# A graph and attention layer on one core: a new opening in which rows are normalised by pairs, TensorE turns most row tiles, and weights load late

## The reference

```
deg = max(count of edges per dst, 1)
xn  = layernorm(x)
x1  = x + (xn @ W1.T + b1 + (segment_sum(xn[src], dst) / deg) @ W2.T + b2)          # graph part
        + (relu(q) . (v_pad^T relu(k)) / normaliser) @ proj.T + proj_bias            # linear attention, 16 heads
          with q, k, v = xn @ qkv_weight.T
x2n = layernorm(x1)
pooled = softmax-weighted mean of x2n over all rows ; the gate picks 2 of 8 experts from it
out = x1 + sum over the 2 experts of g * gelu(gelu(x2n @ w1 + b1) @ w2 + b2)
```

## Time and profile before

| what | value |
|---|---|
| median of three runs | 1469.49 us |
| profiled execution | 1467.96 us, span 1465.9 us |
| busy, of the span | TensorE 93%, VectorE 63%, GpSimd 56%, ScalarE 42% |
| granted TensorE clock, mean | 0.967 |
| first tile's k on TensorE | 21.62 us |
| first gather, last gather issued | 167.7 us, 1156.9 us |

### The profile page before, as it was taken

One profiled execution on the slowest core, in us unless ns is written; L12 is line 12 of the kernel. 1 busy time (PEld: TensorE's weight loads), 2 busy tenths in 40 slices (PEclk: granted clock), 3 DMA queues, 4 the chain that ended last, 5 costly groups with the idle time before them and its releaser, 6 DMA issues.

```text
span 1465.9 us, 22487 instructions
## 1 busy us (share of the span) xinstructions
PE 1364.1 (93%) x7532; PEld 613.0 (42%) x7532; DVE 928.9 (63%) x2122; ACT 622.1 (42%) x1025; POOL 818.7 (56%) x880
## 2 busy tenths in 40 slices
PE   6899999998999999799699699889999889999997
PEld 3454433444444444344244244333434344444443
DVE  7797412115777777577477567746667466776677
ACT  6687412121444444243334234332434336555554
POOL 4542477777677777777777777777777400000000
PEclk9999999999999999899899899989999989999999
DMA  9999799997778787778787777878778541223322
GB/s 271 306 216 222 189 248 250 246 254 231 213 239 254 239 251 239 237 238 254 223 251 240 241 231 238 253 224 251 237 239 250 174 144 39 97 94 114 114 86 100
DMA packets 167029, 309.19 MB, mean 211 GB/s; under 512 B 72019, under 2 KB 74605, under 8 KB 166677
## 3 DMA queue, kind: packets, MB, share of 16 engines
q0 software_dynamic: 62560, 205.05, 47.2%
q1 hardware_dynamic: 36112, 58.90, 12.7%
q10 hardware_dynamic: 68260, 44.01, 11.6%
HBM read 255.02 MB, written 40.02 MB: 201 GB/s over the span
## 4 chain that ended last, share of the span: by engine, by line
PE 37%; POOL 34%; issue 12%; DVE 4%; DMA 1%; ACT 1%; SPq 0%; DVEq 0%; ACTq 0%; POOLq 0%
POOL ring L709 34%; PE bank L755 10%; PE bank L760 10%; PE bank L756 10%; PE bank L826 2%; PE bank L844 1%; PE bank L845 1%; DVE ring L2079 1%; PE bank L956 1%; DMA ring<-table,src_col 1%; PE bank L767 1%; PE bank L967 1%; PE bank L1005 0%; DVE work L2089 0%; DMA b1t<-in_L_ffn_b 0%
## 5 line engine op out<-in xcount | busy, mean ns | idle before, releaser
L709 POOL DMA_INDIRECT ring<-table,src_col x782 | 748.6, 957 | 255.7 <-issue 249.9
L755 PE MATMUL bank<-wts,xT 128*128 128x512 f16 x588 | 225.9, 384 | 13.4 <-DMA xT<-xT 5.7
L756 PE MATMUL bank<-wts,xT 128*128 128x512 f16 x588 | 226.1, 385 | 0.0
L826 PE MATMUL bank<-ring,hot 128*32 128x512 f16 x1560 | 123.8, 398 | 57.1 <-DMA ring<-table,src_col 51.8
L755 PE MATMUL bank<-wts,work 128*128 128x512 f16 x392 | 154.5, 394 | 2.0 <-ACT work L1297 1.4
L756 PE MATMUL bank<-wts,work 128*128 128x512 f16 x392 | 153.8, 392 | 0.0
L760 PE MATMUL bank<-wts,xT 128*128 128x512 f16 x588 | 152.9, 383 | 0.0
L1186 ACT ACTIVATE units<-bank 128x512 f16<-128x512 f32 x65 | 38.8, 598 | 212.0 <-PE bank L826 147.7
L1589 DVE SCALAR_TENSOR_TENSOR units<-bank,units 128x512 f16<-128x512 f32 x65 | 44.8, 689 | 124.0 <-ACT units L1186 123.2
L760 PE MATMUL bank<-wts,work 128*128 128x512 f16 x392 | 102.5, 385 | 0.0
L1718 DVE TENSOR_TENSOR work<-work 128x512 f16<-128x512 f32 x28 | 19.4, 692 | 125.8 <-ACT work L1251 125.8
(11 more groups left out here) (290 smaller groups left out, 2554.6 us busy)
## 6 DMA issues: line engine op xcount, KB each, us to landing
x_rows<-work ACTq DMA_DIRECT2D x51, 256.0 KB
ring<-table,src_col POOLq DMA_INDIRECT x782
work<-in_x ACTq DMA_DIRECT2D x48, 256.0 KB
ring<-x_rows SPq DMA_DIRECT2D x12, 1024.0 KB, 5.1
out_x<-ring SPq DMA_DIRECT2D x12, 1024.0 KB
table<-xT SPq DMA_DIRECT2D x45, 256.0 KB, 4.6
ring<-in_x SPq DMA_DIRECT2D x42, 256.0 KB, 4.1
xT<-in_L_mix_qkv_weight SPq DMA_DIRECT2D x2, 1024.0 KB, 10.1
```

What stands on the lines that cost most here:

```text
L709: pool.indirect_dma_start(ring[:, k, :], None, table[:, :], bass.IndirectOffsetOnAxis(ap=ap, axis=0)).then_inc(sem, 16)
L755: mm(out_, wh(c), mh(c), start=first and c == 0, stop=False)
L756: mm(out_, wh(c), ml(c), start=False, stop=False)
L826: r = mm(ps_unit[a:a + WIDE, :], hot[:, u % 2, DEEP * j + k, :], ring[:, slot(n, j), h * D:(h + 1) * D], start=(k == 0 and h == 0), stop=( ...
```

## The change

- **Rows by pairs.** `normalize(q)` handles two tiles; of 25 pairs, four are handled in three values of i, not three, and all are normalised at i = 17 (before: i = 22). ScalarE writes only `xn32`; the high half is now a cast on GpSimd (`high_half`); columns that were written each time are set once by memsets.
- **Turning.** Tiles 0 to 21 and every even one after are turned by TensorE (8 transposes of 128 x 128 f16 into one bank, 36 tiles) and copied by ScalarE in one 128 x 1024 instruction. The 13 others are turned by DMA as before, now from SyncE's queue.
- **Weights.** Only Wk is loaded at the start. Wv and Wq are loaded behind the last row tile, W1 and W2 after the lists of edges, the projection when the last k is done, and each is turned into its own storage ("in place"). Their 18 steps stand at i = 19 ... 43. The subtraction of a column moves from GpSimd to VectorE. The steps of the edges move from i = 8 ... 13 to i = 6 ... 12 and the lists are made at i = 15.
- **Banks.** All turning of tiles, all weight steps and the sums of tiles in the opening share bank 6, with waits between them.
- **Means via DRAM.** Of the tiles 0 to 27 the mean is stored to DRAM and fetched again three tiles ahead of its use (`spill`, `fetch`), so 10 tiles, not 4, are summed before the first layer.
- **Planner.** Gathers are expected from i = 20 (before: 26), with new constants. Worked out from the two planners: 41 steps and 9 tiles in the opening, 4 steps and one tile between, 150 steps in the rest (before: 29 and 3, 4 and 1, 162).

```diff
-XI = 6
+XI = 8
+XN = 4
+WRITE = 3
+LEAD = 2
+PAIRS = (T + 1) // 2
-KP = 20
-LISTS = 17
-FIRST = 26
+KP = 17
+FIRST = 20
+TURNED = 22
+FLOATS, DIFFERENCES, LEAST, FIRSTS, LISTS = (4, 5), 6, 7, 8, 13
+WEIGHTS_FROM = 19
-K_AT, K_STEP, M_PART, LAYER, GATHERS, LANDING, ADDING = 9.5, 5.7, 5.0, 13.6, 5.05, 4.0, 0.5
+K_AT, K_STEP, M_PART, LAYER, GATHERS, LANDING, ADDING, UNITING = 10.0, 5.8, 5.0, 12.4, 5.05, 4.5, 0.55, 1.6
+def by_pe(t):
+    return t < TURNED or t % 2 == 0
+def pairs_until(i):
+    return min(PAIRS + 2, LEAD + 4 * (i + 2) // 3)
...
# SyncE's queue
             for t in range(XI, T + XI):
                 r = t - XI
-                    sp.wait_ge(s["xn_made"], t - XI + 1)
-                    sp.wait_ge(s["hi_made"], t - XI + 1)
+                    sp.wait_ge(s["xn_made"], r + 1)
                 ...
                 sp.wait_ge(s["hi_made"], r + 1)
                 sp.wait_ge(s["lo_made"], r + 1)
                 stored(sp, r - NS)
+            weight(WV, qkv_w[2 * D:3 * D])
+            weight(WQ, qkv_w[0:D])
+            sp.wait_ge(s["steps_act"], EDGES_ALL)
+            weight(G1, gw1)
+            weight(G2, gw2)
+            def spill(t):
+                sp.wait_ge(s["ah_made"], t + 1)
+                after(sp, s["mean_stored"], 16 * t)
+                sp.dma_start(spilled[t * P:(t + 1) * P, :], mean_in(t)).then_inc(s["mean_stored"], 16)
+            def fetch(t):
+                sp.wait_ge(s["mean_stored"], 16 * t + 16)
+                after(sp, s["turned_ah"], t - WRITE + 1)
+                after(sp, s["mean_loaded"], 16 * t)
+                sp.dma_start(mean_out(t), spilled[t * P:(t + 1) * P, :]).then_inc(s["mean_loaded"], 16)
...
# GpSimd
+            def high_half(t):
+                pool.wait_ge(s["xn_made"], t + 1)
+                pool.tensor_copy(natural(t)[:, 0:D - 1], xn32[:, t % XN, 0:D - 1]).then_inc(s["hi_made"], 1)
-            less_last(WV, 0)
-            less_last(WV, 1)
-            for i in range(KP + 1):
+            for i in range(-1, KP + 1):
                 ...
+                for q in pairs_at(i):
+                    for t in pair(q - 1):
+                        high_half(t)
...
# TensorE
+            def turn_tile(t):
+                pe.wait_ge(s["hi_made"], t + 1)
+                pe.wait_ge(s["lo_made"], t + 1)
+                for c in range(2 * C):
+                    r = nc.tensor.transpose(tile_bank[:, c * P:(c + 1) * P], natural(t)[:, c * P:(c + 1) * P], ident16[:])
+                r.then_inc(s["tile_turned"], 1)
             for i in range(-1, T + 2):
                 ...
+                if i + 1 < T and by_pe(i + 1):
+                    after(pe, s["tile_copied"], turned)
+                    after(pe, s["ah_made"], kept)
+                    after(pe, s["dg_made"], kept)
+                    if n > EDGES_ALL:
+                        pe.wait_ge(s["steps_act"], n)
+                        pe.wait_ge(s["steps_dve"], n)
+                    turn_tile(i + 1)
...
# ScalarE
-            def normalize(n):
+            def normalize(q):
+                for t in pair(q - 1):
+                    act.wait_ge(s["nmr_made"], q)
+                    after(act, s["lo_made"], t - XN + 1)
+                    F(xn32[:, t % XN, :], xin[:, t % XI, :], ACT.Identity, ...).then_inc(s["xn_made"], 1)
+                if pair(q):
+                    act.wait_ge(s["mv_made"], q + 1)
+                    F(std4[:, q % 2, 0:n, 0], mv4[:, q % 2, 0:n, 1], ACT.Sqrt, ...).then_inc(s["std_made"], 1)
-                    F(natural(t)[:, 0:D - 1], xin[:, t % XI, 0:D - 1], ACT.Identity, bias=nmr[:, t % 2], scale=rstd2[:, t % 2])
-                    act.dma_start_transpose(xT[:, t, :, :], natural(t)).then_inc(turned[t % 3], 16)
+            def copy_tile(t):
+                copied[0] += 1
+                act.wait_ge(s["tile_turned"], copied[0])
+                after(act, s["g_made"], t - OFF + 1)
+                stored(act, t - OFF)
+                F(xT[:, t].rearrange("p a n -> p (a n)"), tile_bank, ACT.Copy).then_inc(s["tile_copied"], 1)
-            for i in range(-1, T):
-                if i >= 0:
-                    turn(i + 2)
+            for i in range(-1, T + 2):
+                if i + 1 < T and by_pe(i + 1):
+                    copy_tile(i + 1)
                     act.wait_ge(s["k_made"], i + 1)
                     F(k32, k_bank(i)[:, :], ACT.Relu, scale=SK).then_inc(s["k32_made"], 1)
...
# VectorE
+            def normalize(q):
+                b = (q - 1) % 2
+                if pair(q - 1):
+                    dve.wait_ge(s["std_made"], q)
+                    link(V.reciprocal(rstd4[:, b], std4[:, b]))
+                    V.scalar_tensor_tensor(out=nmr[:, b, 0:n], ...).then_inc(s["nmr_made"], 1)
+                for t in pair(q):
+                    dve.wait_ge(x_loaded[t % XI], ...)
+                    link(V.bn_stats(st12[:, t % 2], xin[:, t % XI, :]))
+                    r = V.bn_aggr(mv4[:, q % 2, t % 2], st12[:, t % 2])
+                for t in pair(q - 2):
+                    dve.wait_ge(s["xn_made"], t + 1)
+                    dve.wait_ge(s["hi_made"], t + 1)
+                    V.tensor_tensor(natural(t)[:, D:2 * D - 1], xn32[:, t % XN, 0:D - 1], natural(t)[:, 0:D - 1],
+                                    ALU.subtract).then_inc(s["lo_made"], 1)
```

More of the change, by code:

```diff
@@ L133, with done_by @@
 assert 0 < REST <= DEEP and STEP * (WINDOWS - 1) - DRIFT >= P * (T - 1) and WINDOWS == LANES * UNITS + 1
+def done_by(i):
+    return max((t for t in SEQ[:i] if t not in LATE), default=-1)
 def step_plan():
-    plan, done, issued = {}, [], [0.0]
-    now = K_AT
+    plan, whole, done, issued = {}, {}, [], [0.0]
+    now, summed = K_AT, -1
     def arrives(n):
@@ L146, in arrives, with take @@
         return issued[n + 1] + LANDING
-    def take(at, room, need):
+    def take(at, room, need=0):
         nonlocal now
@@ L187, in step_plan @@
         take(("end", p), room_, need)
[L188 to L193, removed]
+    assert len(done) == STEPS_SUM
+    return plan, whole
+PLAN, WHOLE = step_plan()
+TILES_K = {i: WHOLE["k", i] for i in range(FIRST, T + 2) if WHOLE["k", i] is not None}
+M_TILE = WHOLE["m", 2]
+AHEAD = {i: WHOLE[i] for i in range(1, T)}
+SPILLED = max([t - WRITE for i, t in AHEAD.items() if t is not None and t - WRITE > done_by(i)], default=0) + 1
@@ L205, with weight_steps @@
-READY = {WV: ("rows_ready", 1), WQ: ("rows_ready", 2), G1: ("weights_ready", 1), G2: ("weights_ready", 2)}
-ORDER = [s for i in sorted(STEPS) for s in STEPS[i]]
-STEPS_ALL = len(ORDER)
-def norm_slots(i):
-    n = LEAD + 2 * (i + 1)
-    return range(n, min(n + 2, T + 2))
[L216 to L220, removed]
-    for k, first in enumerate(RAW):
-        if k and first <= s < first + C:
-            return ORDER.index((k, C - 1)) + 1
-    return ORDER.index(("first", 2)) + 1 if EDGES <= s < RAW[G2] else 0
+def weight_steps():
+    at, i = {}, WEIGHTS_FROM
+    for step in WEIGHT_STEPS:
+        while i in TILES_K:
+            i += 1
+        at[i] = step
+        i += 1
+    assert i <= T
+    return at
@@ L411, in program @@
         slow_loaded = [ctx.enter_context(nc.semaphore(f"slow_loaded{k}")) for k in range(SR)]
-        turned = [ctx.enter_context(nc.semaphore(f"tile_turned{k}")) for k in range(3)]
         block = ctx.enter_context(nc.Block())
@@ L750, in _, with three @@
             mm = nc.tensor.matmul
-            def three(out_, wh, wl, mh, ml, n, first=True, last=True, low=None):
+            def three(out_, wh, wl, mh, ml, n, first=True, last=True, lows=None):
                 for c in range(n):
@@ L922, in _ @@
             query(0)
+            pe.wait_ge(wk_loaded[0], 32)
+            after(pe, s["tile_copied"], turned)
+            after(pe, s["ah_made"], kept)
+            after(pe, s["dg_made"], kept)
+            turn_pj(0, bank[6])
             pe.wait_ge(s["gt_copied"], 5)
@@ L1279, in _ @@
                 unit_high(u)
-            keep_ah(SKEW)
+            if M_TILE is not None:
+                keep_ah(M_TILE)
             def x2T_high(t):
```

544 lines of the change are left out of this document (296 added, 248 removed).

## The result

| | kernel before | changed kernel | forecast |
|---|---|---|---|
| time, median of 8 runs each on one chip | 1469.27 us | 1473.06 us | 1436.6 us |
| ratio of the two, 95% interval | | 1.0025, 1.0014 to 1.0035 | 0.978 |
| span of the profiled execution | 1465.9 us | 1471.2 us | 1433.0 us |
| first gather | 167.7 | 143.0 | 134.8 |
| first to last gather | 989.2 | 1012.9 | 989.2 |

The change makes the kernel slower by 0.25% (0.14% to 0.35%): just outside the 0.2% that can be told from no change. GpSimd does begin 24.7 us earlier, but its gathers then take 23.7 us longer and what follows them 6.3 us longer: -24.7 + 23.7 + 6.3 = +5.3 us, the difference of the spans.

The account below looks back on a forecast made before the run. GpSimd's sequence of gathers was taken as the bound: first gather 134.8 + gathers 989.2 + what follows 309.0 = 1433.0 us span, 1436.6 us as median time; own range 1426 to 1448, wider range 1426 to 1458 at 0.8.

Parts of the forecast that it names:

- rival 3: Turning on TensorE: transposes don't overlap, eight cost 1.76 us, 22 us over 17 tiles, 1459 us; chance 0.05.
- the page's rule: Turning on TensorE: the skill's about 275 ns per transpose, eight cost 2.2 us, 30 us more before the gathers, some 1466 us.
- rival 4: Gather phase: DMA transfers of spilled means crowd the gathers, 48 us if all delays them, 1485 us; chance 0.05.
- rival 2: Bank 6, shared by turned tiles, weight steps and sums, makes TensorE 40 us late, GpSimd loses 25, 1462 us; chance 0.09.
- The edges' steps ... stay covered: Opening: the edges' steps end at i = 15 and, with the lists, stay covered by the table's end.
- 5.87 us for each i: Opening on TensorE: 5.17 for matmuls, 0.45 for turning, 0.25 for edge steps make 5.87 us, against 5.99 before.
- rival 1: VectorE bounds the opening as low halves stretch beside GpSimd: 20 us by i = 16, 1457 us; chance 0.13.
- From the last store to the first gather: End of opening: last row, store and landing keep 10.9 us up to the first gather, expected at 134.8 us.
- GpSimd's column subtraction: Weights: the subtraction fits VectorE's idle time behind i = 17, four of some 2 us and three searches of 2.3, costing nothing.
- Gather phase kept at 989.2: First to last gather: GpSimd's gathers stay the bound at 989.2 us, TensorE keeping 47 us of slack.
- The forecast's 15 us of ring and plan: Gather phase: ring and plan can take 15 us of TensorE's lateness before GpSimd loses time.
- Tail kept at 309.0: Behind the last gather's issue: what follows stays at 309.0 us.

Follow-up runs that it names:

- e14: On e9, each spilled mean is stored a second time to a tensor nobody reads (28 stores, 7.3 MB more): 1454.6 us, ratio 0.9884.
- e2: On the changed kernel, the planner's first number K_AT goes from 10.0 to 0.0, and no sum at i = 49: 1469.5 us, ratio 0.9997.
- e13: On e9, from i = 4 on every pair of rows is normalised one pair sooner: 1455.3 us, ratio 0.9898.
- e1: On the changed kernel, Wv and Wq load during the opening, GNN weights only after i = 21 and 23: 1465.5 us, ratio 0.9969.
- e3: On the changed kernel, ScalarE, not VectorE, subtracts the weights' last column; VectorE's search stands behind units' low halves: 1464.4 us, ratio 0.9963.
- e9: On the changed kernel, moved loads, subtraction on ScalarE and no three extra steps in layer 48, together: 1451.1 us, ratio 0.9880.
- e8: On the changed kernel, one planner condition so that layer 48 does not ask for three steps in piece 3: 1466.8 us, ratio 0.9983.

## Why the prediction was wrong

**What held.** Eight f16 transposes take 0.44 us; from the timeline around one turning:

```profile
104.06 0.61 PE L978 MATMUL bank<-ident,xT 128*128 128x128 f16 x8
104.50 0.38 PE L849 MATMUL bank<-wts,xT 128*128 128x512 f16 x1
```

so rival 3 and the page's rule beside it fall (one such matmul is listed with 0.22 us, but eight start 0.055 us apart). The waits for transposed tiles are gone. That k of tile 4 starts at 48.1, where 47.3 was forecast, is in part luck: k of tile 0 starts at 28.15, 6.5 us later than before and outside my bounds of 2 to 6 (the ten warming matmuls took 3.75 us and not 2.2, at a granted clock of 0.58 from 22 to 28 us), and from there to tile 4 are 19.9 us, not 21.3, since nothing ran at the half clock (1.00 from 28 us on). Seven us for each i behind the first gather was right where nothing stalls (24 of the 28 take 169 us). No cost of the spills was seen; rival 4 at its full price falls by e14. Bank 6 is no bound: rival 2 falls by TensorE's one wait of 0.4 us for it, where it had 40. GpSimd's sequence sets the time: k of tile 48 13 us earlier gave 4 us in e2, while what shortened the gathers' sequence or the end came out as time.

**Steps that failed**, in us of the 38.2:

1. *"The edges' steps ... stay covered"* and 5.87 us for each i: +4.4. k of tile 4 starts 0.8 us late, and i = 5 to 16 took 6.17 each, 74.05 in all. Twelve with a turning alone (5.62, as i = 14) are 67.4, so the seven edge steps cost 6.6 us and not 3.0; 2.3 of it is one idle piece of TensorE at 76.4 us, before the first `src` step. GpSimd's conversion for that step was done at 63.0. The step also waits (`steps_dve`) for a signal that VectorE gives at L1642, and VectorE gives it at 76.3, behind two low halves and its search for the least. So this is rival 1 on a small scale: I had read that a cast on GpSimd stretches no low half, but here their median is 0.812 us and the longest 1.73 (0.681 before); the one at 73.88 took 1.10 beside a cast alone, and in the kernel before one at 83.36 had already taken 0.79 so. The 37 low halves between 50 and 134 us take 8 us more than at 0.681 each. VectorE (third engine of the windows below) is busy 74.9 of these 84 us, where my 4.4 of 5.87 make 63, and e13 shows that it has no room. TensorE waited 2.3 us for it, not 20, and the 3.6 us that I had added for VectorE at the end were enough. The idle piece, VectorE at that time, its low halves, and the windows:

```profile
76.43 0.63 PE L894 MATMUL bank<-ident,wts 128*128 128x128 f32 x4 [2.34 <-issue]
76.42 0.17 DVE L1620 RECIPROCAL rstd<-std 128x2 f32<-128x2 f32 x1 [0.26 <-DVEq L1642]
...
L1635 DVE TENSOR_TENSOR xT<-ring,xT x45: 672/812/1725, 22.5 to 128.7; 128x511 f16<-128x511 f32 x45
...
50.00:100.00 50.00, 47.66 (x281) 25.15 (x280) 46.64 (x93) 32.30 (x53) 39.37 (x44) 1.00 0.73 232
100.00:134.00 34.00, 33.63 (x194) 16.73 (x193) 28.29 (x68) 19.67 (x31) 20.48 (x25) 1.00 0.53 176
```

2. *From the last store to the first gather*, kept at what it was: +3.8 (landing 1.1 less, issue 5.2 more, the rest 0.3 less). I never asked what the weights, moved to right behind the last store, would stand in front of: 3.2 us by e1, the delay of an instruction packet. The other 2.0 go with that packet itself, which the kernel before doesn't need at this place.
3. *"... so does GpSimd's column subtraction, which leaves for VectorE's idle time behind i = 17"*, costed at nothing. VectorE's time was idle, but not free: its two-input instruction stops the gathers. Long gathers are 10.1 us more, 5 of them from the three subtractions; and VectorE's 4.6 us for each weight held TensorE up 7.6 us. Together worth 9 us by e3.
4. *Gather phase kept at 989.2:* GpSimd was blocked 7.4 us more up to 390 us. The forecast's 15 us of ring and plan were right in size, but used up: the gathers came 10 us later than the new plan's clock has them, and TensorE waited 12.0 us for them, and 12.9 us for VectorE's low halves of units, in a stretch where I had counted none, and went on at the lower clock. My own figures had TensorE read k of tile 20 some 10 us behind the first gather, and the planner's first two numbers, 10.0 and 5.8, put it at 15.8. The moved loads, the subtraction on ScalarE and the mended end leave 4.2 us of blocking in e9.
5. *Tail kept at 309.0*, and the last gather free: +10.7 (4.4 in the gathers' phase, 6.3 in the tail). The diff's planner asks in layer 48 for steps that nothing there uses, since the sum it would serve is left to the end part. This could be read from the plan's numbers. Worth 6 us by e8, 9 by its profile.
6. The rest, 1.8 us, is in gathers each up to 0.1 us longer.

(4.4 + 3.8 + 10.1 + 7.4 + 10.7 + 1.8 = 38.2.) With the three causes mended the span is 1446.3, 13.3 above the forecast: 4.2 at the first gather, 5.3 in the gathers, 3.8 in the tail. So the change's idea was worth most of what its first gather says: in e9 it comes 28.6 us earlier than before, and 18 us of that are time. What the change moved gave the gain back.

Open: why GpSimd needs a packet of instructions behind its branch now and needed none before, why the tail of the best run is still 3.8 us longer than before, and how much of the planner's phase is still lost in it.

## What to carry to other kernels

Work that is moved to an idle engine or an idle queue is free only if nothing shares what it uses: look at what a moved load stands in front of (here a packet of instructions, over the same DMA engines, came 3.2 us later behind weight loads) and at whether a VectorE instruction has two SBUF inputs while GpSimd issues gathers. A plan written from estimated times must be checked against the trace of the kernel that it is in: where its clock starts, in which piece of a layer units end, and what it demands at the last layer. When a change removes 25 us at the head and the time does not move, take the sequence that sets the time apart, instruction by instruction; here three sums (long, blocked, rest) and the two ends held all of it.

## Not expected of the hardware

- A gather issued 0.09 us behind a 2.28 us two-input VectorE instruction took 3.01 us; beside a one-input one of 2.29 us, 0.95.
- GpSimd stood 3.0 us at a branch with idle DMA engines, 6.1 to 6.2 us with 2 to 4 MB of loads issued around it; in all these runs the first gather came 2.0 to 2.1 us after the start of one 8 KB instruction packet. It stood 0.97 us in the kernel before, with no such packet, where it had stood idle for 12 us ahead of it (153.6 to 165.5).
- After waits of 3.5 to 7.6 us TensorE's matmuls stood 0.43 us apart, not 0.22, for 3 to 5 us, at a granted clock of 0.50.
